# Attention 0 with heads gathered in one PSUM bank, a shared ring of banks and a gated output projection; attention 1 with wide masks and its bias added by GpSimd

## The chip, the cores and the metric

The kernel runs on one core of a Trainium2 chip. The metric is the device time of one launch in microseconds (us), lower is better. TensorE is called PE, VectorE DVE, ScalarE ACT, GpSimd POOL and SyncE SP.

## The reference, cut to what matters

Sixteen batches of 256 tokens with 128 features pass two layers; each layer is an attention and a feed-forward part, both with modulated layer norms and gated residuals. The change lies in the two attentions.

```
mod = (silu(L0_c) @ L0_wmod)...            # sa, ca, ga, sb, cb, gb per batch
h = layernorm(x) * (1 + ca) + sa
q = h @ Wq + bq;  latent = h @ Wl + bl;  k = latent @ Wk + bk;  v = latent @ Wv + bv
attn = softmax(q k^T * 8**-0.5)            # attention 0: 16 heads of 8 features
x = x + ga * (attn v @ Wo + bo)
x = x + gb * ffn0(...)                     # then layer 1:
attn = softmax(causal(q k^T)); A_mem = ... # attention 1: 4 heads of 32 features
x = x + ga1 * ((g * A_mem + (1 - g) * attn v) @ Wo.T + bo)
x = x + gb1 * mixture_of_experts(...)
```

## The kernel before

The program is a row of blocks: `prepare`, `attention0`, the feed-forward part of layer 0, `attention1`, the expert part. Between blocks all engines meet at a barrier. X stays in SBUF.

`attention0` is a software pipeline written by hand. Step n (0 to 19) has 16 slots; each engine runs its own program with the same steps and slots, and the order in it is fixed by the tables `PES`, `DVE` and `ACTS`. In step n the engines work on several batches at once: f = n (layer norm turned by `pe_ln`, projections `pe_qk` and `pe_v`), m = n - 2 (the maxima), s = n - 3 and t = n - 4 (scores, exponentials, values, output). One slot of PE (`pe_tiles`) is one tile of maxima (two matmuls into one of the two banks `p_max`, read by DVE's `dve_max_tile`) and one half of a transposed score tile (two matmuls into `p_sT`, read by ACT's `act_exp`). At slot 0 of step n the maxima's wait asks that the operands of batch n - 2 stand in `QK` (semaphore `stacked`, all 12 transfers of that batch and of those before it).

Those operands are made so: `act_qk` writes q and k, ACT and POOL (`pool_parts`) split them in three bf16 parts, and SP copies the parts from SBUF to SBUF with 12 DMAs of 64 KB (`sp_stack`, the stack of a batch below). The maxima of batch s go the other way round: DVE splits them (`dve_negmax`, slot 0), PE turns them (`pe_max_turn`, slot 2), ACT copies (`act_maxT`), SP copies them into `QK` with 2 DMAs (`sp_max`), and the scores of s, from slot 6 on, need them.

SP's program per step is `sp_max(n - 3)`, one group of feed-forward weights, `sp_stack(n)`. SP is a queue in order: a wait in it holds back all that stands behind it.

The output of batch t: `pe_pv` (four groups of heads, each 4 heads x 2 key tiles, into 4 x 32 partitions of `p_o`), `act_OT` four times, `pe_turn_O` twice, `dve_normalise_O` twice, `pe_turn_back`, `act_OTn`, `pe_out`, `act_y` (gate and bias per feature), `pe_turn_y`, `dve_add`. All but `p_o` share the bank `p_m`.

`attention1` has one step per batch, PE's order being scores, turn_a, out, logits, turn_b, turn_c, mem, q and k, v, pv, layer norm. `pe_out` adds the gated bias with a matmul of one row behind each projection.

Of the kernel before, what the change touches and what calls it, by code (L numbers as in the profile page):

```python
# [22 lines left out]
P = 128  # L23
# [20 lines left out]
PES = {"ln": 0, "max_turn": 2, "qk": 3, "O0": 5, "v": 8, "O1": 9, "back": 11, "out": 12, "turn_y": 14,  # L44
       "pv_s": (11, 15), "pv_t": (3, 7)}
DVE = {"negmax": 0, "stats": 2, "O0": 6, "O1": 10, "add": 15}
ACTS = {"hT": 0, "maxT": 1, "qk": 3, "v": 7, "OTn": 11, "y": 12, "OT_s": (11, 15), "OT_t": (3, 6)}
# [75 lines left out]
def prepare(nc, k, a):  # L123
    with ExitStack() as ctx:
# [24 lines left out]
        zeroed = sem("zeroed")  # L149
        ident_ready = sem("ident_ready")  # L150
# [50 lines left out]
        def _(pool):  # L201
# [8 lines left out]
            for r in range(NB):  # L210
                pool.memset(k.V[r][:, :, :, DH0 + 1:], 0.0)
                if r >= 2:
                    pool.memset(k.QK[r][:, :, 1, :], 1.0)
# [34 lines left out]
        def _(dve):  # L248

            for r in range(NB):  # L250
                dve.memset(k.V[r][:, :, :, DH0:DH0 + 1], 1.0)
                if r < 2:
                    dve.memset(k.QK[r][:, :, 1, :], 1.0)
            dve.wait_ge(small_loaded, SMALL)
# [58 lines left out]
def late_loads(k, a):  # L313
# [4 lines left out]
    loads.append((k.bo1[:], a["L1_attn_bo"].rearrange("(o d) -> o d", o=1)))  # L318
# [11 lines left out]
def attention0(nc, k, a):  # L330
    with ExitStack() as ctx:
        sb, ps, sem = tensors(nc, ctx, "att0")
        QK, V = k.QK, k.V
        stats = sb("stats", [P, NT, 6])
# [13 lines left out]
        OT = [sb(f"OT{n}", [P, S]) for n in range(4)]  # L348
        recip = sb("recip", [P, 2, NT, 4])
        O = sb("O", [P, NT, H0, DH0])  # L350
        OTn = sb("OTn", [P, S])
        yT = sb("yT", [P, S])
# [8 lines left out]
        p_o = ps("p_o", [P, 512])  # L361
        p_m = ps("p_m", [P, 512])
        p_m16 = p_m[:].bitcast(BF16)

        stats_step = sem("stats_step")
# [14 lines left out]
        scored = sem("scored")  # L380
        maxed = sem("maxed")
# [9 lines left out]
        O_turned = sem("O_turned")  # L391
        recip_ready = sem("recip_ready")
        O_ready = sem("O_ready")
        OTn_turned = sem("OTn_turned")
        OTn_ready = sem("OTn_ready")
        y_made = sem("y_made")
        yT_ready = sem("yT_ready")
        y_turned = sem("y_turned")
        x_added = sem("x_added")

# [9 lines left out]
        STACK_DMAS = 2 * len(TERMS)  # L410

# [5 lines left out]

        def head_rows(w, n):
            return slice(w * HALF, w * HALF + n)


        def pe_ln(pe, b):
            pe.wait_ge(xn_ready, b + 1)
            at_least(pe, v_ready, b)
            at_least(pe, x_added, b - 4)
# [4 lines left out]
        def pe_qk(pe, b):  # L430
            pe.wait_ge(hT_ready, b + 1)
            at_least(pe, maxT_ready, b - 2)
            pe.matmul(p_m[:, 0:S], k.wq0[:], hT[:], start=True, stop=True)
            pe.matmul(p_m[:, S:2 * S], k.wk0[:], hT[:], start=True, stop=True).then_inc(qk_made, 1)

        def pe_v(pe, b):
            pe.wait_ge(qk_ready, b + 1)
            at_least(pe, O_ready, 2 * (b - 4) + 1)
# [4 lines left out]
        def pe_tiles(pe, max_of, scores_of):  # L443

            if max_of is not None:
                b, r, u = max_of
                if u == 0:
                    pe.wait_ge(stacked, 16 * STACK_DMAS * (b + 1))
                at_least(pe, maxed, TILES * b + u - 1)
# [6 lines left out]
            for i in range(NT):  # L456
                if max_of is not None:
                    rows = head_rows(w, MAXROW)
                    mm = pe.matmul(p_max[u % 2][:, i, :], QK[r][rows, g, 0, i * P:(i + 1) * P], QK[r][rows, g, 1, :],  # L459
                                   start=True, stop=True)  # L460
                    if i == NT - 1:
                        mm.then_inc(scored, 1)
# [7 lines left out]
        def pe_max_turn(pe, b):  # L470
            pe.wait_ge(neg_ready, b + 1)
            if not isinstance(b, int) or b + 3 < B:
                wait_apart(pe, k, hT_ready, b + 4)
            else:
                at_least(pe, x_added, b - 1)
# [5 lines left out]
        def pe_pv(pe, b, r, g):  # L481
            if g == 0:
                pe.wait_ge(v_ready, b + 1)
            pe.wait_ge(exped, PAIRS * b + 2 * g + 2)
            at_least(pe, OT_ready, 4 * b + g)
            for j in range(NT):
                for h in range(4):
                    mm = pe.matmul(p_o[32 * h:32 * h + 32, 0:S], V[r][:, j, 4 * g + h, :],  # L488
# [391 lines left out]

# [1306 lines left out]
```

## Time and profile before

| | us |
|---|---|
| median of 3 runs | 896.36 (893.45 to 896.53) |
| the profiled execution's own time | 895.1 |
| its span | 893.3 |
| `prepare`, up to about | 21 |
| attention 0, about | 21 to 342 |
| feed-forward 0, about | 342 to 568 |
| attention 1 and its router, about | 568 to 742 |
| experts, about | 742 to 893 |

Over the whole span PE is busy 83%, DVE 69%, ACT 63% and POOL 40%. These are means over stages with different limits; what holds a stage is read from that stage's own rows.

### The profile page before, as it was taken

To read this page: it belongs to the slowest core of one execution; us is meant where nothing else is said; L and a number is where in the kernel's file an instruction comes from. 1 tells how busy PE (TensorE), PEld (TensorE's weight loads), DVE (VectorE), ACT (ScalarE), POOL (GpSimd) and SP (SyncE) were. 2 spreads that over 40 slices of the span, in tenths; PEclk is the share of its full clock that TensorE was granted. 3 is DMA by queue.
4 is the path that set the end of the run, shared out by engine and by line. 5 is a ranking of instruction groups with operands and counts; after the bars stand their busy time and mean duration, and the time that the engine had idled before them with its cause. 6 is when DMAs were issued, how large, how long until landed. Compare 5 with 4: busy or idle time off the path is not lost. (4 is left out here: it accounts for less than half of the span.)

```text
span 893.3 us, 17728 instructions
## 1 busy us (share of the span) xinstructions
PE 743.3 (83%) x5927; PEld 538.4 (60%) x5927; DVE 613.4 (69%) x1483; ACT 563.2 (63%) x1258; POOL 359.6 (40%) x449
## 2 busy tenths in 40 slices
PE   3376888888888874789999997589999967999996
PEld 3222444444444334789889997367777755888784
DVE  3075777777777835677877763367767856888884
ACT  0214777777777753668878886277677734565553
POOL 3542534534421001051121000477877643777674
PEclk9999999999999985899999999599999987999998
DMA  5355354443442001300000000000000060464430
GB/s 138 47 73 73 64 67 66 66 68 52 55 54 41 2 3 14 119 1 2 1 1 1 1 1 1 2 2 1 2 1 3 18 176 4 112 187 114 118 107 23
DMA packets 76927, 42.05 MB, mean 47 GB/s; under 512 B 9026, under 2 KB 74916, under 8 KB 76580
## 3 DMA queue, kind: packets, MB, share of 16 engines
q1 hardware_dynamic: 76836, 40.89, 22.9%
q8 instruction: 51, 0.84, 0.4%
q14 instruction: 40, 0.33, 0.2%
HBM read 25.66 MB, written 2.24 MB: 31 GB/s over the span
## 5 line engine op out<-in xcount | busy, mean ns | idle before, releaser
L579 DVE TENSOR_REDUCE att_negmax<-att_p_max 128x2 f32<-128x512 f32 x256 | 164.6, 685 | 74.2 <-PE att_p_max L459 73.2
L663 ACT ACTIVATE att_probs<-att_p_sT 128x1024 f32<-128x1024 f32 x128 | 129.3, 1022 | 47.1 <-PE att_p_sT L465 46.1
L2047 POOL TENSOR_TENSOR moe_z_lo<-moe_z,moe_z_hi 128x512 fp32r<-128x512 f32 x64 | 96.6, 1524 | 54.8 <-ACT moe_z_hi L2000 53.0
L459 PE MATMUL att_p_max<-att0p_QK 48*128 48x256 bf16 x512 | 91.6, 288 | 26.9 <-DVE att_negmax L579 11.4
L939 POOL TENSOR_TENSOR ffn0s_rstd<-ffn0s_var_eps,top_minus_half 128x2 f32<-128x2 f32 x16 | 11.2, 698 | 197.3 <-DVE ffn0s_var_eps L926 197.3
L465 PE MATMUL att_p_sT<-att0p_QK 51*128 51x256 bf16 x512 | 86.0, 281 | 0.2 <-DMA att0p_QK<-att_maxT 0.2
L893 PE MATMUL ffn0s_p_h<-ffn0s_u_hi,top_ffn_all 128*128 128x256 f32 x256 | 70.9, 309 | 16.5 <-DVE ffn0s_u_lo L1154 16.2
L459 PEld LDWEIGHTS att_p_max<-att0p_QK 48*128 48x128 bf16 x512 | 33.2, 96 | 77.3 <-DVE att_negmax L579 46.8
L488 PE MATMUL att_p_o<-att_probs,att0p_V 128*32 128x256 f32 x1024 | 70.5, 394 | 10.0 <-ACT att_probs L663 9.0
L1154 DVE TENSOR_TENSOR ffn0s_g_lo<-ffn0s_g,ffn0s_g_hi 128x512 fp32r<-128x512 f32 x64 | 49.0, 781 | 42.0 <-ACT ffn0s_g_hi L1098 40.7
L2038 DVE TENSOR_TENSOR moe_z<-moe_act_u,top_ffn_all 128x512 f32<-128x512 f32 x64 | 73.5, 1149 | 2.2
L1751 POOL TENSOR_SCALAR att_prob<-att_prob,att_rsums 128x256 f32<-128x256 f32 (+1 forms) x128 | 56.0, 455 | 38.2 <-DVE att_rsums L1656 38.1
L1094 ACT ACTIVATE ffn0s_g<-ffn0s_p_h,top_ffn_scales 128x256 f32<-128x256 f32 x128 | 54.5, 486 | 23.2 <-PE ffn0s_p_h L894 22.9
L750 POOL TENSOR_TENSOR att_rstd<-att_var_eps,top_minus_half 128x2 f32<-128x2 f32 x16 | 11.5, 719 | 141.0 <-DVE att_var_eps L572 141.0
L894 PE MATMUL ffn0s_p_h<-ffn0s_u_lo,top_ffn_all 128*128 128x256 f32 x256 | 67.0, 294 | 0.0
L893 PEld LDWEIGHTS ffn0s_p_h<-ffn0s_u_hi,top_ffn_all 128*128 128x128 f32 x256 | 52.1, 203 | 22.2 <-DVE ffn0s_u_lo L1154 15.8
L2017 ACT ACTIVATE moe_act_g<-moe_p_g 128x512 f32<-128x512 f32 x64 | 38.3, 599 | 38.6 <-PE moe_p_g L897 38.6
L893 PE MATMUL ffn0s_p_h<-ffn0s_g_hi,top_ffn_all 128*128 128x256 f32 x256 | 62.0, 283 | 0.0
L894 PE MATMUL ffn0s_p_h<-ffn0s_g_lo,top_ffn_all 128*128 128x256 f32 x256 | 60.9, 279 | 0.0
L2033 DVE TENSOR_TENSOR moe_act_u<-moe_act_g,moe_p_u 128x512 f32<-128x512 f32 x64 | 43.6, 681 | 21.4 <-PE moe_p_u L897 18.7
L1098 ACT ACTIVATE ffn0s_g_hi<-ffn0s_p_h,top_ffn_scales 128x256 fp32r<-128x256 f32 x128 | 54.8, 497 | 0.0
L1563 ACT ACTIVATE att_prob<-att_p_s,att_negmax 128x256 f32<-128x256 f32 (+1 forms) x128 | 52.1, 427 | 3.0 <-DVE att_negmax L1669 2.7
(248 smaller groups left out, 2037.5 us busy)
## 6 DMA issues: line engine op xcount, KB each, us to landing
top_ffn_all<-combine SPq DMA_DIRECT2D x32, 512.0 KB, 6.9
att0p_QK<-att_parts SPq DMA_DIRECT2D x192, 64.0 KB
top_X<-in_L_attn_x SPq DMA_DIRECT2D x4, 512.0 KB, 6.9
att_raw<-in_L_ffn_h_w SPq DMA_DIRECT2D x8, 256.0 KB, 2.8
out_x<-top_X SPq DMA_DIRECT2D x8, 256.0 KB, 2.3
top_wo_all<-gates SPq DMA_DIRECT2D x1, 1024.0 KB, 5.2
ffn0s_raw_gu<-in_L_ffn_w SPq DMA_DIRECT2D x1, 1024.0 KB, 8.0
prep_wmod<-in_L_wmod SPq DMA_DIRECT2D x2, 384.0 KB, 3.7
```

The source lines that it names most:

```text
L459: mm = pe.matmul(p_max[u % 2][:, i, :], QK[r][rows, g, 0, i * P:(i + 1) * P], QK[r][rows, g, 1, :], start=True, stop=True)
L465: mm = pe.matmul(p_sT[t % 2][:, sw, i, :], QK[sr][rows, t, 1, i * P:(i + 1) * P], QK[sr][rows, t, 0, :], start=True, stop=True)
L488: mm = pe.matmul(p_o[32 * h:32 * h + 32, 0:S], V[r][:, j, 4 * g + h, :], probs[g % 2][:, h // 2, h % 2, j, :], start=(j == 0), stop=(j == ...
L579: dve.tensor_reduce(negmax[:, :, w, g], p_max[u % 2][:], AX.X, ALU.max, negate=True).then_inc(maxed, 1)
L663: act.activation(probs[g % 2][:, t % 2], p_sT[t % 2][:], ACT.Exp).then_inc(exped, 1)
L893: pe.matmul(out, w_hi, x_hi, start=first, stop=False)
L894: mm = pe.matmul(out, w_hi, x_lo, start=False, stop=last and w_lo_is_zero)
L1094: act.activation(g[q][:, m, :], p_h[q][:, m, :], ACT.Gelu, scale=k.ffn_scales[:, layer, 2 * q + m:2 * q + m + 1])
L1098: ins = act.activation(g_hi[r][:, 2 * q + m, :], p_h[q][:, m, :], ACT.Gelu, scale=k.ffn_scales[:, layer, 2 * q + m:2 * q + m + 1])
L1751: ins = pool.tensor_scalar(prob[b % 2][:, h, at], prob[b % 2][:, h, at], rsums[:, i, h:h + 1], 0.0, ALU.mult, ALU.add)
L2038: dve.tensor_tensor(z[e % RING][:], act_u[e % 2][:], k.cb[u % 2][:, e, :], ALU.mult).then_inc(z_ready, 1)
L2047: pool.tensor_tensor(z_lo[e % RING][:], z[e % RING][:], z_hi[e % RING][:].bitcast(F32), ALU.subtract).then_inc(z_lo_ready, 1)
```

## The change

Attention 0. Two heads now share a block of 32 columns of V: the second one's values stand at columns 8 to 15, their ones at column 17, and two groups of heads are summed into the same PSUM rows, so that `p_o` holds all 16 heads in one bank. One `act_OT`, one `pe_turn_O` and one `dve_normalise_O` replace four, two and two. The two banks `p_max` become a ring that also takes the turned outputs and the projection (semaphores `filled` and `drained` instead of `scored` and `maxed`), so DVE reads all its PSUM data there. The output projection is token-major: Wo times the gate of the batch is prepared ahead (`pool_gate_wo`), the gated bias is added to X by POOL (`pool_bias`), and `act_y` and `pe_turn_y` are gone. The gates go through DRAM once more, in attention 0 (`pe_turn_gates`, `act_gate_rows`, loads of 4 batches in SP's steps 1 to 4). The tables are rewritten: `pe_max_turn` moves from slot 2 to slot 3 and now waits for `OTn_ready`, the scores of s begin at slot 8 instead of 6, the last part of the output moves to a step of its own (y = n - 5), and there are 21 steps instead of 20. SP's step becomes `sp_max(n - 3)`, `sp_stack(n - 1)`, gates, weights (from step 5 on).

Attention 1. `pe_out` loses its bias matmuls, POOL adds the gated bias to X in `pool_norm1`, and each head's mask is one matmul of 256 columns over both diagonal blocks instead of two of 128.

```diff
-PES = {"ln": 0, "max_turn": 2, "qk": 3, "O0": 5, "v": 8, "O1": 9, "back": 11, "out": 12, "turn_y": 14,
-       "pv_s": (11, 15), "pv_t": (3, 7)}
+PES = {"back": 1, "max_turn": 3, "out": 5, "ln": 6, "q": 9, "k": 10, "v": 13, "O": 14,
+       "pv_s": {14: (0, 0), 15: (0, 1)}, "pv_t": {2: (1, 0), 3: (1, 1), 6: (2, 0), 7: (2, 1), 10: (3, 0), 11: (3, 1)}}
+SCORES = 8
...
         def pe_max_turn(pe, b):
             pe.wait_ge(neg_ready, b + 1)
...
+            at_least(pe, OTn_ready, b - 1)
+            pe.wait_ge(v_ready, min(b + 3, B))
...
+        def pe_turn_O(pe, b):
+            at = RING["O", b]
+            pe.wait_ge(OT_ready, b + 1)
+            at_least(pe, drained, at - 1)
+            for i in range(NT):
+                for half in range(2):
+                    mm = pe.transpose(bank(at)[:, i, half * P:(half + 1) * P], OT[:, half, i * P:(i + 1) * P], k.ident[:])
+            mm.then_inc(filled, 1)
...
         def pe_out(pe, b):
+            at = RING["out", b]
             pe.wait_ge(OTn_ready, b + 1)
-            pe.matmul(p_m[:, 0:S], k.wo0[:], OTn[:], start=True, stop=True).then_inc(y_made, 1)
...
+            for i in range(NT):
+                mm = pe.matmul(bank(at)[:, 0, i * D:(i + 1) * D], OTn[:, i * P:(i + 1) * P], k.wo1_all[:, b, :],
+                               start=True, stop=True)
...
+        def dve_normalise_O(dve, b):
...
+            dve.reciprocal(recip[:], groups[:, :, 2 * DH0:2 * DH0 + 2]).then_inc(recip_ready, 1)
...
+            dve.tensor_tensor(O[:].rearrange("p i (m g d) -> p (i m) g d", g=2, d=DH0),
...
+        def act_OT(act, b):
+            act.wait_ge(pv_made, 4 * b + 4)
...
+            act.activation(OT[:], p_o[:], ACT.Copy).then_inc(OT_ready, 1)
...
-        def sp_step(sp, n, r):
+        def sp_step(sp, n):
             if batch_valid(n - 3):
-                sp_max(sp, n - 3, (r - 3) % NB)
-            if 0 <= n - 1 < WEIGHT_GROUPS:
...
+                sp_max(sp, n - 3, (n - 3) % NB)
+            if batch_valid(n - 1):
+                sp_stack(sp, n - 1, (n - 1) % NB)
...
+            g = n - FIRST_GROUP
+            if 0 <= g < WEIGHT_GROUPS:
...
-            if batch_valid(n):
-                sp_stack(sp, n, r)
...
+        def pool_bias(pool, b):
+            x = k.X[:, b * NT:(b + 1) * NT, :]
...
+            pool.tensor_tensor(x, x, k.gbo1_all[:, b, :].unsqueeze(1).to_broadcast([P, NT, D]), ALU.add).then_inc(bias_added, 1)
...
-                pe.matmul(out, OT[b % 2][:, i * P:(i + 1) * P], k.wo1_all[:, b, :], start=True, stop=False)
-                mm = pe.matmul(out, k.ones_row[0:1, :], k.gbo1_row[0:1, b, :], start=False, stop=True)
+                mm = pe.matmul(out, OT[b % 2][:, i * P:(i + 1) * P], k.wo1_all[:, b, :], start=True, stop=True)
```

The order of SP's queue before, around step 8 of attention 0 (QK3 is the stack of batch 7, QK0 that of batch 8; QK1 and QK2 with maxT are the maxima of batches 5 and 6; the names of semaphores of an earlier block are those of numbers used again):

```order
L732 DMA att0p_QK3<-att0_parts1 8x8x512 x2
L712 DMA att0p_QK1<-att0_maxT 3x8x256 [waits prep_s_bo_made,att0_s_maxT_ready]
L712 DMA att0p_QK1<-att0_maxT 3x8x256
L742 DMA att0_raw1<-in_L0_ffn_h2_w 128x512 [waits att0_s_w_lo_ready,att0_s_w_loaded]
L732 DMA att0p_QK0<-att0_parts0 8x16x256 [waits prep_s_wl_turned,prep_s_bv_ready,att0_s_scoredT]
...
L732 DMA att0p_QK0<-att0_parts0 8x8x512 x2
L712 DMA att0p_QK2<-att0_maxT 3x8x256 [waits prep_s_bo_made,att0_s_maxT_ready]
```

And in the changed kernel around its step 9:

```order
L745 DMA att0p_QK3<-att0_parts1 8x8x512 x2
L768 DMA att0_raw0<-in_L0_ffn_h1_w 128x512 [waits att0_s_w_lo_ready,att0_s_w_loaded]
L768 DMA top_ffn_scales<-in_L0_ffn_h2_s 128x4x1
L725 DMA att0p_QK2<-att0_maxT 3x8x256 [waits att0_s_maxT_ready]
L725 DMA att0p_QK2<-att0_maxT 3x8x256
L745 DMA att0p_QK0<-att0_parts0 8x16x256 [waits prep_s_bias_made,att0_s_stacked,att0_s_scoredT]
...
L745 DMA att0p_QK0<-att0_parts0 8x8x512 x2
```

The stack of batch 8 (QK0) stood ahead of the maxima of batch 6 (QK2) and now stands behind them.

The start of a step on PE, in the changed kernel, step 9 (m = 7 in QK3, t = 5 in QK1):

```order
L481 MATMUL att0_p_max1<-att0p_QK3 128x256 [waits att0_s_exped,att0_s_drained,att0_s_stacked]
L487 MATMUL att0_p_sT0<-att0p_QK1 128x256
...
L528 MATMUL att0_p_m<-top_ident,att0_O 128x128 [waits att0_s_v_ready,att0_s_drained]
L528 MATMUL att0_p_m<-top_ident,att0_O 128x128
...
L509 MATMUL att0_p_o<-att0_probs1,att0p_V1 32x256 [waits att0_s_exped]
L509 MATMUL att0_p_o<-att0_probs1,att0p_V1 32x256 x3
L497 MATMUL att0_p_m<-top_ident16,att0_negparts 48x128 [waits att0_s_v_ready,att0_s_OTn_ready,att0_s_neg_ready]
L497 MATMUL att0_p_m<-top_ident16,att0_negparts 48x128
```

The turning of the maxima (L497) has moved behind slot 2, behind the turning back of the output (L528, whose copy by ACT it waits for) and behind half a group of values (L509). Before, the same step began so:

```order
L427 MATMUL att0_p_m<-top_ident,att0_xn 128x128
L459 MATMUL att0_p_max0<-att0p_QK3 128x256 [waits att0_s_exped,prep_s_gate_step,prep_s_bv_ready]
L465 MATMUL att0_p_sT1<-att0p_QK1 128x256
...
L477 MATMUL att0_p_m<-top_ident16,att0_negparts 48x128 [waits att0_s_neg_ready,prep_s_c_tanh]
L477 MATMUL att0_p_m<-top_ident16,att0_negparts 48x128
```

In both, the first maxima matmul of a step waits for the stack of its batch; what moved is when that stack is issued.

## Rows read from the trace of the kernel before

**Rows 1.** Step 9's window, length, busy PE, PEld, DVE, ACT, POOL, PEclk, DMA, GB/s.
```profile
166.66:183.32 16.66, 14.25 (x156) 6.88 (x154) 12.96 (x33) 12.68 (x20) 7.05 (x8) 1.00 0.45 69
```

**Rows 2.** SP's queue in time: start, length, line, what; steps 9 and 10.
```profile
168.54 1.53 SPq L712 DMA_DIRECT2D att0p_QK<-att_maxT  x2
172.65 9.13 SPq L732 DMA_DIRECT2D att0p_QK<-att_parts  x12
185.21 1.53 SPq L712 DMA_DIRECT2D att0p_QK<-att_maxT  x2
```

**Rows 3.** SP's queue in the first steps.
```profile
29.62 8.50 SPq L732 DMA_DIRECT2D att0p_QK<-att_parts  x12
38.16 0.45 SPq L742 DMA_DIRECT2D att_raw<-in_L_ffn_w_w  x1
44.37 8.44 SPq L732 DMA_DIRECT2D att0p_QK<-att_parts  x12
57.98 7.93 SPq L732 DMA_DIRECT2D att0p_QK<-att_parts  x12
66.02 1.96 SPq L712 DMA_DIRECT2D att0p_QK<-att_maxT  x2
72.36 8.53 SPq L732 DMA_DIRECT2D att0p_QK<-att_parts  x12
85.21 1.54 SPq L712 DMA_DIRECT2D att0p_QK<-att_maxT  x2
```

**Rows 4.** SP's own waits, 29 to 90 us: sum, times, longest.
```profile
SPq L732 <- DMA att0p_QK<-att_parts: 11.9, 3, 5.2
```

**Rows 5.** PE in the first steps, where it sat idle for a transfer.
```profile
44.40 0.61 PE L459 MATMUL att_p_max<-att0p_QK 48*128 48x256 bf16 x4 [6.87 <-DMA att0p_QK<-att_parts]
73.02 0.37 PE L459 MATMUL att_p_max<-att0p_QK 48*128 48x256 bf16 x1 [8.01 <-DMA att0p_QK<-att_maxT]
```

**Rows 6.** ACT at the start of step 9.
```profile
167.23 1.02 ACT L663 ACTIVATE att_probs<-att_p_sT 128x1024 f32<-128x1024 f32 x1
168.15 0.36 ACT L656 ACTIVATE att_maxT<-att_p_m 48x256 bf16<-48x256 bf16 x1
```

**Rows 7.** PE's longest idle stretch in the drain.
```profile
314.51 0.29 PE L477 MATMUL att_p_m<-top_ident,att_negparts 128*48 128x128 bf16 x2 [3.47 <-DVE att_negparts L591]
```

**Rows 8.** Windows behind it; the granted clock is the third figure from the end.
```profile
316.00:318.00 2.00, 1.99 (x12) 0.85 (x8) 0.00 (x0) 1.60 (x3) 0.00 (x0) 0.50 0.04 12
320.00:322.00 2.00, 1.95 (x16) 0.85 (x8) 0.00 (x0) 1.07 (x2) 0.00 (x0) 0.50 0.00 0
```

**Rows 9.** DMA strip of 181 to 187 us: busy tenths in 40 slices of 0.15 us.
```profile
DMA  5676656667666584466532110000000000003110
```

**Rows 10.** ACT's maxima copy in step 17, and DVE at the end of attention 0.
```profile
298.25 0.36 ACT L656 ACTIVATE att_maxT<-att_p_m 48x256 bf16<-48x256 bf16 x1
...
340.69 0.27 DVE L797 TENSOR_REDUCE att_lo_flag<-att_lo_row 1x1 f32<-1x128 f32 x1 [2.01 <-DMA att_lo_row<-flag]
```

**Rows 11.** Groups of one step of attention 0: busy us, mean ns | idle before.
```profile
L668 ACT ACTIVATE att_OT<-att_p_o 128x256 f32<-128x256 f32 x4 | 1.5, 378 | 0.4 <-PE att_p_o L488 0.3
L498 PE MATMUL att_p_m<-top_ident,att_OT 128*128 128x128 f32 x8 | 1.3, 286 | 0.3 <-ACT att_qk L642 0.3
L514 PE MATMUL att_p_m<-top_ident,att_yT 128*128 128x128 f32 x2 | 0.4, 300 | 0.1
```

**Rows 12.** POOL groups of one step of attention 1 (639.9 to 649.3 us).
```profile
L1751 POOL TENSOR_SCALAR att_prob<-att_prob,att_rsums 128x128 f32<-128x128 f32 (+1 forms) x8 | 3.5, 457 | 2.0 <-DVE att_rsums L1656 2.0
L1777 POOL TENSOR_TENSOR w_h_lo<-att_hT,w_h_hi 128x256 fp32r<-128x256 f32 x1 | 0.7, 724 | 0.1
```

**Rows 13.** PE in one step of attention 1, in time.
```profile
640.84 0.48 PE L1500 MATMUL att_p_n<-top_gbo_row,top_ones_row 1*128 1x128 f32 x2
641.25 0.61 PE L1421 MATMUL att_p_n<-top_wg,att_hT 128*128 128x8 f32 x4
```

**Rows 14.** Window of one step of attention 1, columns as in Rows 1.
```profile
640.42:649.78 9.36, 9.01 (x85) 7.00 (x84) 6.61 (x28) 6.88 (x25) 7.16 (x14) 1.00 0.01 2
```

More of the change, by code:

```diff
@@ L416, in weights_loaded, with bank @@
             return 16 * sum(len(g) for g in weight_loads[:groups])
+        RING = {}
+        for n in range(LAST):
+            for slot in range(TILES):
+                if slot == PES["out"] and batch_valid(n - 5):
+                    RING["out", n - 5] = len(RING)
+                if slot == PES["O"] and batch_valid(n - 4):
+                    RING["O", n - 4] = len(RING)
+                if batch_valid(n - 2):
+                    RING["max", n - 2, slot] = len(RING)
+        def bank(at):
+            return p_max[at % 2]
         def head_rows(w, n):
@@ L479, in pe_max_turn @@
             mm.then_inc(max_turned, 1)
[L481 to L488, printed above, removed]
-                                   probs[g % 2][:, h // 2, h % 2, j, :], start=(j == 0), stop=(j == NT - 1))
-            mm.then_inc(pv_made, 1)
@@ L517, in pe_step @@
         def pe_step(pe, n, r):
-            f, m, s, t = n, n - 2, n - 3, n - 4
+            f, m, s, t, y = n, n - 2, n - 3, n - 4, n - 5
             rm, rs, rt = (r - 2) % NB, (r - 3) % NB, r
             for slot in range(TILES):
+                if slot == PES["back"] and batch_valid(y):
+                    pe_turn_back(pe, y)
+                if slot == PES["max_turn"] and batch_valid(s):
+                    pe_max_turn(pe, s)
+                if slot == PES["out"] and batch_valid(y):
+                    pe_out(pe, y)
@@ L620, in dve_step @@
-                if slot == DVE["O0"] and batch_valid(t):
-                    dve_normalise_O(dve, t, 0)
-                if slot == DVE["O1"] and batch_valid(t):
-                    dve_normalise_O(dve, t, 1)
+                    neg_chain(dve, s)
+                if slot == DVE["out"] and batch_valid(y):
+                    dve_add(dve, y)
+                if slot == DVE["O"] and batch_valid(t):
+                    dve_normalise_O(dve, t)
                 if batch_valid(m):
@@ L627, in dve_step @@
                     dve_stats(dve, f + 1)
-                if slot == DVE["add"] and batch_valid(t):
-                    dve_add(dve, t)
         def act_hT(act, b):
@@ L843, in _ @@
         def _(pe):
[L844 to L849 removed]
+            pe_turn_gates(pe)
+            for n in range(LAST):
                 pe_step(pe, n, n % NB)
```

379 lines of the change are left out of this document (180 added, 199 removed).

## The prediction

> **What bounds the kernel now.** I read the share of busy time by stage first, then one step of attention 0, then SP's queue, because the change rewrites that queue's order. A step in the steady part lasts 16.66 us and PE is busy 14.25 us of it, DVE 12.96, ACT 12.68 and POOL 7.05 [rows 1]. So PE is the nearest to full, none is full, and a step can be bound by PE's work with DVE's and ACT's short waits, or by a chain that no engine's busy time shows. The reader should look at the transfers next. SP issues the two transfers of the maxima at 168.54 and again at 185.21, which is the period, and between them the 12 transfers of a stack from 172.65, in 9.13 us [rows 2]. In the kernel before, a stack has the rest of its own step and the whole next one before PE wants it, so its flight costs nothing there.
>
> How long a stack flies can be seen where nothing else covers it, at the start. SP issues the first at 29.62; the second waits by its own code for the first to land and leaves at 44.37, the third at 57.98, the fourth at 72.36 [rows 3], and these are the three waits for such a transfer in SP's own waits [rows 4]. PE starts its first maxima at 44.40, released by the same transfers [rows 5]. So a stack takes 14.75, 13.61 and 14.38 us from first issue to landing, mean 14.2, though its issue lasts only 8 to 8.5 us. In each case a group of weights was issued right behind it [rows 3], as it will be in the changed kernel from step 5 on.
>
> **The change, part by part.**
>
> *The stack's place in SP's queue.* Before, step n issues the stack of batch n, wanted at slot 0 of step n + 2. Now step n + 1 issues it, behind the maxima's transfers of that step, wanted again at slot 0 of step n + 2. SP can't issue the stack until ACT has copied the turned maxima. That closes a loop of one step: slot 0, turning of the maxima, ACT's copy, 2 transfers issued, 12 transfers issued and landed, slot 0 of the next step. Its length:
>
> - From slot 0 to the end of ACT's copy. Before, step 9 starts at 166.6, where the window of [rows 1] does, and the copy ends at 168.51 [rows 6]: 1.9 us. Now the turning stands one slot later, behind half a group of values, and waits for ACT's copy of the output, which stands behind an exponential of 1.02 us [rows 6] that itself needs slots 0 and 1. I count: slots 0 and 1 with the turning back 0.9, to the exponential 0.1, exponential 1.0, copy of the output 0.4, turning 0.4, copy of the maxima 0.4: 3.2 us.
> - The two issues, 1.53 us [rows 2], with the gap behind them 1.6.
> - The stack, 14.2 us.
>
> Sum 19.0 us, against 16.67 between the two maxima's issues in [rows 2]. PE's own work is about 13 us in it, so it idles in one piece for 3 us or more. After an idle of 3.47 us in the drain [rows 7] the granted clock stands at 0.50, that is 1.2 instead of 2.4 GHz, in the windows from 316 to 322 [rows 8]. If that happens in every step, slots 0 to 3 take up to 1 us more, in part of the steps. I take 19.2 us for a step.
>
> Bounds of the stack's flight: below, the end of traffic instead of the landing. The strip of 181 to 187 us goes to zero at slice 22 to 27 of 0.15 us, about 184.4 to 185.1 [rows 9], 12.4 us after 172.65; I use 12.6. Above, 15.2, since steps 1 to 4 also load 512 KB of gates behind each stack. I take 14.2 because it is a landing, and the landing is what PE waits for.
>
> The Trainium skill (DMA: Bandwidth & Descriptors, on the two cost components of a transfer) gives a fixed cost of about 2 us for a DMA plus its bytes over 436 GB/s. An estimate by that page lets the last of the 12 transfers land about 2.2 us after its issue, the stack after 10.6 us and the loop after 15.4 us, so nothing would wait for it. In [rows 3] the landing comes 13.6 to 14.8 us after the first issue, so the trace disagrees where it can be seen.
>
> Steps 4 to 16 are 13 steps of the loop. Before, the maxima's transfers of step 4 leave at 85.21 [rows 3], and ACT's copy of step 17 ends at 298.61 [rows 10]: 213.4 us. Now 13 x 19.2 = 249.6. **Plus 36.2 us.**
>
> *The start.* Before, PE sat idle 8.01 us in step 3 for the maxima's transfers [rows 5], since these were issued at 66.02 behind the third stack [rows 3]; that goes. Against it, steps 2 and 3 run the loop too, cold, and the second stack waits for the store and the loads of the gates: about 61 us for step 3's start, 67 for the third stack's issue, 81 to 82 for its landing. Step 4 then issues its maxima's transfers at about 85. **0 us**, between -5 and +2.
>
> *Work taken from PE, ACT and DVE in attention 0.* Half of the 8 turnings, 0.65 us, and the turning of y, 0.4; three of four copies of 378 ns and the scaling, about 1.5 us of ACT; about 0.5 us of DVE [rows 11]. POOL gains a bias add of about 0.73 us (the 128x256 row in [rows 12]), on an engine busy 7 of 16.7. All of it lies beside the loop, so it is worth nothing in steps 4 to 16. If the loop did not bind, it would be worth up to 1.1 us of PE in a step. In the drain there is one step more, but its slots are nearly empty and the chain from last values to X is shorter by the scaling and its turning. Before, the stage ends with the flag at 340.69 [rows 10]. **Minus 1.5 us**, between -3 and +2.
>
> *Attention 1.* A bias matmul pair holds PE from 640.84 to 641.25 [rows 13], 0.41 us, and there are two in each of 16 steps: 13.1 us. PE is busy 9.01 of 9.36 us in a step [rows 14], so it is PE's time. The wide masks give about 0.1 us a step. POOL is busy 7.16 us of 9.36 and waits 2.0 us for DVE; with the add of 0.72 [rows 12, 14] it reaches 7.9 to 8.2, against a step of about 8.5. It stays just behind PE, but it takes part of the gain where it doesn't. DVE's add now waits for POOL's, which is made three steps ahead of it, so that wait is covered; without the lead it would cost at most POOL's 0.7 a step. **Minus 11 us**, between -4 and -14.
>
> Sum: 36.2 + 0 - 1.5 - 11 = +23.7 us. The profiled execution took 895.1 us, 1.3 under the median of the runs; I add the difference to both, and give the median: 896.4 + 23.7, about **920 us**.
>
> **The rivals.**
>
> *The stack is hidden (faster).* If it landed about 2 us after its last issue, the loop would be 4.8 + 10.6 = 15.4 us, and PE and DVE would set about 15.5. Then 13 x 15.5 = 201.5 is 11.9 less than before, and the sum -11.9 - 1.5 - 11 gives 872. It speaks for this that the last part of a stack shared the engines with weights at the start; against it, three landings that agree, and traffic to 12.4 us in the steady part, where no weights were behind the stack. It decides at a flight under 11.9 us, where the loop equals 16.7.
>
> *It lands when traffic ends (no change).* Flight 12.6, step 17.4, 13 steps 226.2, +12.8 - 1.5 - 11: 897.
>
> *PE cold in every step (slower still).* The clock falls in each pause, slots 0 to 3 take 1.2 us more, and gates or weights stretch the stack by 0.3: step 20.5, 266.5, +53 - 1.5 - 11: 937.
>
> *The change's gains in attention 1 don't come* because POOL becomes its bound: -4 instead of -11, 927. It lies in the likeliest one's range.
>
> **How the numbers follow.** The likeliest, the loop with a flight near 14.2 us, has 0.68, and its own range, with the last rival in it, is 908 to 930. The cold one has 0.08, the traffic's end 0.10, the hidden stack 0.14. Leaving out the hidden one and some of the cold one, the range is 895 to 937. A measurement of this kernel tells about 0.5%, 4.5 us, from no change. Slower by more than that: 0.68 + 0.08 + 0.02 of the third, 0.78; within it 0.08; faster 0.14.
>
> **What would show it.** In the profile after, PE's first maxima matmul of each step waits for the stack's transfer, 2 to 5 us, 13 times or so; SP's maxima's issues lie 19 us apart; the stack's first issue comes right behind them and about 4.8 us after PE's slot 0; DVE and ACT wait for PE in one long piece a step, and PE's clock falls in some. A step of attention 1 is 8.5 us. I am wrong if the issues are 16 us apart or less, or if PE's slot 0 waits for something else. That would mean that the landing at the start isn't that of the steady part.

## Result: slower by 3.6%, and the profile after

The changed kernel takes 927.26 us (median of 4 runs, 922.44 to 934.43) against 896.41 for the kernel before on the same chip. The ratio is 1.036, with a 95% interval of 1.028 to 1.044. The profiled execution took 924.53 us, with a span of 922.8 against 893.3. All medians and ranges below are of all runs of a version, but the ratios leave out runs of a slower state, which are five of the ten of the version with half of the stack on GpSimd's queue and one of the four with GpSimd's splitting.

The page of the changed kernel gives the busy times and the strip of PE's granted clock, in tenths, one digit for 1/40 of the span:

```profile
PE 765.3 (83%) x5738; PEld 516.2 (56%) x5738; DVE 633.5 (69%) x1423; ACT 538.8 (58%) x1195; POOL 390.3 (42%) x484
...
PEclk9998886779797886679999999979999996999998
```

PE has 189 matmuls fewer than before and is busy 22 us longer. That is only possible at a lower clock, and the strip says where: mostly in slices 4 to 18 (69 to 415 us), which are attention 0 from its step 3 on and the first 30 us of what follows.

SP's queue shows the step, with the columns of [rows 2]:

```profile
104.42 1.56 SPq L725 DMA_DIRECT2D att0p_QK<-att_maxT  x2
106.09 8.01 SPq L745 DMA_DIRECT2D att0p_QK<-att_parts  x12
...
124.84 1.56 SPq L725 DMA_DIRECT2D att0p_QK<-att_maxT  x2
126.52 8.02 SPq L745 DMA_DIRECT2D att0p_QK<-att_parts  x12
...
144.39 1.55 SPq L725 DMA_DIRECT2D att0p_QK<-att_maxT  x2
```

The maxima leave 20.4 and 19.6 us apart, where [rows 2] had 16.67. PE, where it idles longest in the same steps:

```profile
100.37 0.39 PE L481 MATMUL att_p_max<-att0p_QK 48*128 48x256 bf16 x1 [2.74 <-DMA att0p_QK<-att_parts]
...
120.79 0.39 PE L481 MATMUL att_p_max<-att0p_QK 48*128 48x256 bf16 x1 [3.77 <-DMA att0p_QK<-att_parts]
...
140.34 0.39 PE L481 MATMUL att_p_max<-att0p_QK 48*128 48x256 bf16 x1 [2.90 <-DMA att0p_QK<-att_parts]
```

So the reader can walk round the loop: slot 0 at 100.37, the maxima's issue at 104.42 (4.05 us later), the stack's first issue at 106.09 (1.67), slot 0 at 120.79 (14.70). The next flight, 126.52 to 140.34, is 13.82. In the 13 steps from 84.94 to 339.86 PE's slot 0 is released by the stack 12 times, with flights of 11.82 to 14.78 us, 13.96 in the mean. PE's waits from 30 to 370 us (line, releaser, sum, times, longest) have it first:

```profile
PE att_p_max L481 <- DMA att0p_QK<-att_parts: 43.8, 15, 9.2
PE att_p_max L481 <- DVE att_negmax L597: 13.8, 31, 2.2
```

The windows of four steps and of the drain have the columns of [rows 1]:

```profile
104.42:124.84 20.42, 16.29 (x152) 6.08 (x150) 13.88 (x28) 11.21 (x16) 7.90 (x9) 0.83 0.44 53
124.84:144.39 19.55, 16.29 (x152) 6.07 (x150) 13.87 (x28) 11.20 (x16) 7.89 (x9) 0.85 0.41 56
144.39:167.22 22.83, 20.39 (x152) 7.05 (x150) 15.04 (x28) 11.31 (x16) 7.77 (x9) 0.65 0.40 48
206.99:223.73 16.74, 14.95 (x156) 5.88 (x158) 13.77 (x29) 11.23 (x17) 7.10 (x10) 0.96 0.36 66
339.86:384.92 45.06, 38.46 (x302) 13.06 (x300) 19.25 (x33) 22.12 (x26) 0.00 (x0) 0.72 0.01 2
```

Steps differ: 16.7 us at a clock of 0.96, 22.8 us at 0.65. The short one had the shortest flight, 11.82 us, and its path from slot 0 to the end of the copy at 223.71, 3.24 us, at full clock:

```profile
208.65 8.13 SPq L745 DMA_DIRECT2D att0p_QK<-att_parts  x12
220.47 0.28 PE L481 MATMUL att_p_max<-att0p_QK 48*128 48x256 bf16 x1 [0.95 <-DMA att0p_QK<-att_parts]
```

The long one is the one step of the 13 in which PE doesn't wait for the stack at slot 0, which it reaches at 161.49. Two slots later it waits for VectorE:

```profile
164.83 0.39 PE L481 MATMUL att_p_max<-att0p_QK 48*128 48x256 bf16 x1 [2.24 <-DVE att_negmax L597]
```

The end of attention 0 and the rows of attention 1's step (line 1511 is once in a step):

```profile
384.92 0.27 DVE L833 TENSOR_REDUCE att_lo_flag<-att_lo_row 1x1 f32<-1x128 f32 x1
```

```profile
652.53 0.60 PE L1511 MATMUL att_p_t<-top_ident,att_prob 128*128 128x128 f32 x4
...
660.38 0.60 PE L1511 MATMUL att_p_t<-top_ident,att_prob 128*128 128x128 f32 x4
```

The accounts by stage: attention 0 ends at 384.92, 44.2 us later than in [rows 10]. Of that the 13 steps from the maxima's issue at 84.94 to that at 339.86 give 254.9 - 213.4 = 41.5, and the drain from there on 3.0. Attention 1, from its first to its last row of line 1511, takes 120.1 us against 133.5 before, 13.4 less. The rest is 1.3 less. Sum +29.5, the difference of the spans.

### The profile page after: what moved, and what is told of

Read it like the earlier page. It is cut to its first block and busy times, and to the rows that moved or that the text cites. A ratio compares the mean times of both kernels' runs of the same rounds, so it can differ in the third digit from the quotient of the medians.

```text
span 922.8 us, 17153 instructions
## 1 busy us (share of the span) xinstructions
PE 765.3 (83%) x5738; PEld 516.2 (56%) x5738; DVE 633.5 (69%) x1423; ACT 538.8 (58%) x1195; POOL 390.3 (42%) x484
## 5 line engine op out<-in xcount | busy, mean ns | idle before, releaser
L597 DVE TENSOR_REDUCE att_negmax<-att_p_max 128x2 f32<-128x512 f32 x256 | 172.4, 690 | 97.4 <-PE att_p_max L481 93.3
L481 PE MATMUL att_p_max<-att0p_QK 48*128 48x256 bf16 x512 | 115.6, 325 | 58.6 <-DMA att0p_QK<-att_parts 43.8
L481 PEld LDWEIGHTS att_p_max<-att0p_QK 48*128 48x128 bf16 x512 | 31.0, 100 | 150.3 <-DVE att_negmax L597 61.1
L487 PE MATMUL att_p_sT<-att0p_QK 51*128 51x256 bf16 x512 | 114.5, 324 | 0.0
L509 PE MATMUL att_p_o<-att_probs,att0p_V 128*32 128x256 f32 x1024 | 102.1, 479 | 0.3 <-ACT att_probs L681 0.3
L898 PE MATMUL ffn0s_p_h<-ffn0s_u_hi,top_ffn_all 128*128 128x256 f32 x256 | 69.5, 305 | 16.6 <-DVE ffn0s_u_lo L1159 16.2
L1099 ACT ACTIVATE ffn0s_g<-ffn0s_p_h,top_ffn_scales 128x256 f32<-128x256 f32 x128 | 54.7, 488 | 23.6 <-PE ffn0s_p_h L899 23.2
```

What stands on the lines that cost most here:

```text
L481: mm = pe.matmul(bank(at)[:, i, :], QK[r][rows, g, 0, i * P:(i + 1) * P], QK[r][rows, g, 1, :], start=True, stop=True)
L487: mm = pe.matmul(p_sT[t % 2][:, sw, i, :], QK[sr][rows, t, 1, i * P:(i + 1) * P], QK[sr][rows, t, 0, :], start=True, stop=True)
L509: mm = pe.matmul(p_o[32 * h:32 * h + 32, g // 2, :], V[r][:, j, (g // 2 * 4 + h) * 2 + g % 2, :], probs[g % 2][:, h // 2, h % 2, j, :], st ...
L597: dve.tensor_reduce(negmax[:, :, w, g], bank(at)[:], AX.X, ALU.max, negate=True).then_inc(drained, 1)
L898: pe.matmul(out, w_hi, x_hi, start=first, stop=False)
L1099: act.activation(g[q][:, m, :], p_h[q][:, m, :], ACT.Gelu, scale=k.ffn_scales[:, layer, 2 * q + m:2 * q + m + 1])
```

## Experiments

**Theory**: a step is the loop of the prediction, closed by the stack standing behind the maxima on SP's queue. **Rival A**: the stack's wait is only where PE's idle time shows, and the new order on PE, the ring of two banks, is the slow part. **Rival B**: a stack is slow wherever it is issued. "Steps 4 to 17" below is always the time from ScalarE's copy of the maxima in step 4 to that in step 17, 13 steps: 213.4 us in the kernel before, 254.9 in the changed one.

**The late stack alone, in the kernel before.**

```diff
-            if batch_valid(n):
-                sp_stack(sp, n, r)
+            if batch_valid(n - 1):
+                sp_stack(sp, n - 1, (r - 1) % NB)
```

> The kernel before, with the stack of batch n - 1 instead of n in SP's step n, in the same place behind the maxima's transfers and the weights; nothing else changed. Loop theory: a step becomes 1.9 us to the copy of the maxima, 2.1 for these transfers and the weights' issue, 14.2 for the stack's flight, 18.2 us instead of 16.67. Over 12 to 13 steps that is +18 to +20 us, less up to 5 at the start: 908 to 916 us. Rival, the new slots and the ring make the longer step, not the place of the stack: no change, 896 within 3.

Measured: 904.6 us, ratio 1.011 (1.005 to 1.016): slower, as the loop theory has it, but 3 us under the range that I had given. PE again waits for the stack, in the order of before:

```profile
115.52 0.28 PE L459 MATMUL att_p_max<-att0p_QK 48*128 48x256 bf16 x1 [0.89 <-DMA att0p_QK<-att_parts]
...
149.25 0.28 PE L459 MATMUL att_p_max<-att0p_QK 48*128 48x256 bf16 x1 [0.32 <-DMA att0p_QK<-att_parts]
```

Steps 4 to 17 take 227.6 us, 17.5 each. The prediction's sum with the old path to the copy, 1.9 + 1.6 + 14.2, is 17.7. The 17.5 is a mean of unlike steps: four of the 13 take 16.67 or 16.68 us, with no wait for the stack, and the loop hardly exceeds PE's own step here. The move of one call thus costs 14 us there without any change of PE's order (the start gives 5.7 back, since step 4's copy comes at 79.14 instead of 84.82), and the rest of the 41.5 needs the longer path to the copy, or the clock.

**The stack back in its own step, in the changed kernel** (the same edit reversed), and the same with the parts copied at slot 10 in place of 13.

> The changed kernel with the stack of batch n back in SP's step n (wanted two steps later), all slots and the ring as changed. Loop theory: the stack's flight leaves the loop; but the parts are ready only at slot 13, so the stack's issue ends about 21 us after the step's start and holds back the next maxima's transfers, which the scores at slot 8 want; a step of about 17 us instead of 19.6, 890 to 900 us. Rival, the slots and the ring make the longer step: 927 within 5.

> As the run before, and ACT splits off the first parts at slot 10 instead of 13, so that the stack's issue ends before the next maxima are turned. Loop theory: a step of 15.5 to 16 us, bound by PE and DVE, clock at full level again; 13 x (19.6 - 15.7) = 51 less than the changed kernel, 872 to 882 us. Rival, the slots and the ring: 927 within 5.

Measured: 1006.9 us (ratio 1.127) and 976.9 us (1.091), the opposite of what I expected. SP's queue of the first:

```profile
173.50 8.50 SPq L745 DMA_DIRECT2D att0p_QK<-att_parts  x12
...
183.01 1.55 SPq L725 DMA_DIRECT2D att0p_QK<-att_maxT  x2
199.42 8.51 SPq L745 DMA_DIRECT2D att0p_QK<-att_parts  x12
```

and PE between:

```profile
189.49 0.37 PE L481 MATMUL att_p_max<-att0p_QK 48*128 48x256 bf16 x1 [7.44 <-issue]
```

In this order the parts come at slot 13, so the stack leaves as the step ends, and the next step's maxima stand behind its 12 issues. They leave at 183.01, and PE stands 7.44 us before slot 8, where the scores want them (the profile names no releaser, but that transfer is what the code waits for there). The next parts are behind that slot: another loop, of 25 us. Undoing one line of a change is no undoing, since the slots around it had moved. The two say nothing against the theory, but they show that the queue's order, not the number of transfers, decides.

**Two more transfers between the maxima and the stack, in the changed kernel.**

```diff
+            at_least(sp, spared, 32 * b)
+            for w in range(2):
+                sp.dma_start(spare[w * 3 * PAIRS:(w + 1) * 3 * PAIRS, :], maxT[w * 3 * PAIRS:(w + 1) * 3 * PAIRS, :]
+                             ).then_inc(spared, 16)
```

> The changed kernel, with two more transfers of the maxima's size, into a spare tile that nobody reads, on SP's queue between the maxima and the stack in every step. An issue of the maxima takes 0.8 us, so the stack's first issue comes 1.6 us later. Loop theory: the delay goes round the loop, 1.6 us a step in 13 steps (the two of the start and the drain aside), +21 us and more where the clock falls further: 942 to 960. Rival 'the stack is not what sets the step': 922 to 932, the spread of the changed kernel.

Measured: 954.2 us, ratio 1.066 (1.063 to 1.068), 27 us over the changed kernel and in the range I had given. Steps 4 to 17 take 287.3 us, 22.1 each, 2.5 more for a dose (the added delay of the stack's first issue) of 1.6:

```profile
110.95 1.56 SPq L732 DMA_DIRECT2D att_spare<-att_maxT  x2
112.63 8.04 SPq L752 DMA_DIRECT2D att0p_QK<-att_parts  x12
```

```profile
109.35:131.99 22.64, 16.08 (x152) 6.06 (x150) 13.87 (x28) 11.20 (x16) 7.89 (x9) 0.80 0.39 49
131.99:157.07 25.08, 23.11 (x152) 7.89 (x150) 15.08 (x28) 11.53 (x16) 7.77 (x9) 0.57 0.33 45
```

What stands on the queue ahead of the stack is paid in every step: rival A alone falls. The excess over the dose, 0.9 us a step, is half flight and half clock: over the 12 steps that the stack releases the flight is 14.4 us in place of 14.0, and the path from slot 0 to the copy 4.1 in place of 3.7. The one step without such a release, the second window at 0.57, takes 25.1 us.

**The maxima on ScalarE's queue, in the changed kernel.**

```diff
             act.activation(maxT[:], p_m16[0:6 * PAIRS, 0:S], ACT.Copy).then_inc(maxT_ready, 1)
+            act_max(act, b, b % NB)
...
-            if batch_valid(n - 3):
-                sp_max(sp, n - 3, (n - 3) % NB)
```

> The changed kernel, with the two maxima's transfers issued on ScalarE's queue right behind the copy that makes them, so that SP's queue holds only the stack, the gates and the weights and issues each stack as its parts come, some four slots before slot 0 of the next step. Loop theory: the loop maxima, stack, slot 0, turn is cut, TensorE waits for no stack, its clock stays high, and a step takes TensorE's own 15.3 to 15.8 us in place of 19.6: some 13 x 4 = 52 us under the changed kernel, 868 to 880 us. ScalarE gets two issues of about 0.8 us a step, of which some may show. Rival 'the transfers' flight is what costs, wherever it is issued' (they share the queues and land late): 915 to 930. Rival 'TensorE's new order with single-bank ring is the slow part': 915 to 930 as well, but with TensorE waiting for the ring's reads and not for the stack.

Measured: 910.3 us, ratio 1.014 (1.005 to 1.022). After the first stack (9.2 us) PE waits for one 0.4 us in the whole stage, the loop is cut. But the gain is 17 us, not 52. Step 9's window and PE's waits from 60 to 350 us:

```profile
166.79:183.91 17.12, 14.17 (x152) 5.71 (x152) 13.69 (x28) 11.09 (x17) 7.85 (x10) 1.00 0.47 65
```

```profile
PE att_p_max L481 <- DVE att_negmax L597: 35.2, 48, 2.4
PE att_p_max L481 <- DMA att0p_QK<-att_maxT: 6.4, 1, 6.4
```

Steps 4 to 17 take 236.0 us, and they are of two kinds. Nine in a row, from 132.53 to 284.05, are at full clock and take 16.3 to 17.2 us, 16.8 in the mean, not the 15.3 to 15.8 of my expectation. In step 9's window PE idles 1.24 us before slot 2, behind VectorE's splitting of the maxima at the step's start, and 0.98 before slot 8:

```profile
172.74 0.27 PE L481 MATMUL att_p_max<-att0p_QK 48*128 48x256 bf16 x1 [0.98 <-DVE att_negmax L597]
```

VectorE's reads ahead of that slot had ended by 171.92; what that slot still waits for is the maxima's transfer, issued at 167.20. Where the wait at slot 8 is 0.2 us or less the step is 16.3 us, under the 16.67 of before. So rival A holds little: at full clock the new order isn't slower than the old one, and the ring's wait at slot 2 is a part of what keeps it above PE's own time.

The other four steps take 24.6, 19.4, 20.1 and 20.4 us at clocks of 0.50 to 0.81. They account for two thirds of the missing gain, and with them comes something that the kernel before doesn't show in its steady steps. VectorE splits the maxima in four small operations (the chain), whose second and fourth, subtractions, take 0.19 us there each time. Here the chain runs at the same time as GpSimd's splitting of q and k, and some of its operations are stretched:

```profile
181.84 0.19 DVE L609 TENSOR_TENSOR att_negparts<-att_negrest,att_negparts 128x32 bf16<-128x32 f32 x1
...
300.23 1.20 POOL L801 TENSOR_TENSOR att_parts<-att_rest,att_parts 128x512 bf16<-128x512 f32 x1
300.44 1.03 DVE L609 TENSOR_TENSOR att_negparts<-att_negrest,att_negparts 128x32 bf16<-128x32 f32 x1
...
302.13 0.39 PE L481 MATMUL att_p_max<-att0p_QK 48*128 48x256 bf16 x1 [2.23 <-DVE att_negmax L597]
```

The same operation takes 1.03 us in place of 0.19 and ends 0.04 us after GpSimd's. This happens at three step starts (84, 108 and 300 us); PE's wait at slot 2 is then 2.37, 1.74 and 2.23 us in place of 1.24, its next matmul takes 0.39 us in place of 0.28, and the slow steps are those that hold such a start or follow it. That the stretched chain causes them is not shown, since no run moved GpSimd's operations alone.

**GpSimd splits the maxima**, on top of the last: `neg_chain(dve, s)` becomes `neg_chain(pool, n - 3)` at the step's start, with two buffers for the maxima.

> The maxima on ScalarE's queue as before in this series, and the four small operations that split the maxima in parts moved from VectorE to GpSimd, with two buffers for the maxima. It tests what is left of the step there, 17.14 us against 16.67 in the kernel before. If it is VectorE's chain of 1.5 us at the step's start, at which TensorE's ring waits 1.2 us, the step falls to 16.2 to 16.8 us and the time to 895 to 903; if GpSimd brings the chain too late for the turn at slot 3, the wait moves there and the step is 17 to 18 us, 905 to 925; if the wait for the maxima at slot 8 sets it, the step stays at 17.1 and slot 8 waits longer.

Measured: 927.0 us (920.4 to 938.2), ratio 1.035 (1.030 to 1.040), worse. PE waits for the split parts at the turn instead, and the clock is below full in ten of the 13 steps:

```profile
PE att_p_m L497 <- POOL att_negparts L610: 18.9, 14, 1.5
```

```profile
161.91:183.24 21.33, 19.84 (x152) 7.17 (x152) 12.75 (x24) 11.40 (x16) 8.59 (x14) 0.68 0.38 52
```

This step has no wait for a stack and yet lasts 21.3 us: PE is busy 19.84 of it, with the same work that took 14.17 at full clock. It doesn't tell whether the chain on VectorE set the 17.1 us. The three steps at full clock take 18.3 to 18.4 us, over 1 us more than with the chain on VectorE.

**Half of the stack on GpSimd's queue, in the changed kernel.** GpSimd issues the six transfers of the second half of the rows as soon as it has made the parts; SP keeps the maxima and, behind them, the other six.

```diff
-                    for w in range(2):
-                        rows = slice(w * HALF + n * DH0, w * HALF + (n + 1) * DH0)
-                        sp.dma_start(QK[r][rows], term_source(r, w, n)
-                                     ).then_inc(stacked, 16)
+                    rows = slice(n * DH0, (n + 1) * DH0)
+                    sp.dma_start(QK[r][rows], term_source(r, 0, n)).then_inc(stacked, 16)
+
+        def pool_stack(pool, b, r):
+            pool.wait_ge(part2_ready, b + 1)
...
+                pool.dma_start(QK[r][rows], term_source(r, 1, n)).then_inc(stacked1, 16)
```

> The changed kernel, with six of a stack's twelve transfers (the second half of the rows) issued on GpSimd's queue right behind the parts that it makes, a step earlier; the maxima and the other six stay on SP's queue, the maxima ahead. Loop theory: only six transfers stand behind the maxima, issued in 4 us where twelve took 8. If the flight of 14.2 to 14.7 us is made by the issues, it shortens by about 4 us, the loop closes in 15 us and no longer binds; a step is then the 17.1 us that it takes with the maxima on ScalarE's queue: some 2.5 us a step less than the changed kernel, 890 to 905. If the flight is made by the transfers' bytes on shared rings, it stays above 12 us and the time stays at 915 to 930. If GpSimd's queue issues slowly (over 1 us each) its other work comes late and the time is over 930.

Measured: 893.4 us (881.0 to 903.2), ratio 0.991 (0.988 to 0.994): 34 us under the changed kernel. Against the kernel before (896.1 on that chip) it is level or a little faster, by less than its own spread of 22 us. The profiled execution took 896.2. After the first (7.9 us) PE waits for no stack, and the attention's end is at 360.50 in place of 384.92. Its windows:

```profile
104.62:128.17 23.55, 22.28 (x152) 7.82 (x152) 14.19 (x28) 11.53 (x16) 11.85 (x16) 0.58 0.29 48
128.17:144.50 16.33, 14.11 (x152) 5.69 (x152) 13.69 (x28) 11.18 (x16) 10.46 (x13) 1.00 0.37 62
144.50:163.46 18.96, 17.53 (x152) 6.44 (x152) 13.81 (x28) 11.18 (x17) 12.84 (x17) 0.77 0.38 58
```

A step at full clock is 16.3 to 16.6 us, up to 0.3 less than [rows 1]. Rival B falls as the cause of the wait: the same bytes, half of them elsewhere and earlier, are in time. How long they fly isn't seen, since nothing waits for them. Steps 4 to 17 still take 238.2 us, 18.3 each, because in most the clock is below full.

**The same, with SP's half ahead of the maxima** (the two calls in `sp_step` change places).

> The kernel with six of a stack's transfers on GpSimd's queue, and on SP's queue the other six issued ahead of the maxima in place of behind them. Their parts are ready when the step begins and their issues take 4.0 us, about the time until the maxima are ready, so that neither stands behind the other for long. Loop theory: nothing of the stack stays in the loop through the maxima, and the steps that still waited are 16.3 to 16.6 us at full clock: 875 to 893. Rival from the two kernels with the whole stack in its own step, where the maxima landed only with the stack ahead of them: the maxima come late at slot 8, TensorE waits there 1 to 3 us a step, and the time is 895 to 925.

Measured: 965.5 us, ratio 1.079 (1.073 to 1.086). The rival that I had named is right, and larger than I put it:

```profile
127.83 4.82 SPq L747 DMA_DIRECT2D att0p_QK<-att_parts  x6
132.69 1.53 SPq L728 DMA_DIRECT2D att0p_QK<-att_maxT  x2
```

```profile
140.77 0.29 PE L483 MATMUL att_p_max<-att0p_QK 48*128 48x256 bf16 x1 [3.38 <-issue]
```

SP first waits for the last parts. The maxima behind them are issued only 0.3 us after they are ready (132.38), but slot 8 starts about 8 us after that issue, with two halves of a stack in flight: a loop of 23.1 us.

**The weights ahead of the stack, in the changed kernel.**

> The changed kernel, with a step's group of weights issued ahead of the stack in place of behind it. Loop theory: the weights' issues delay the stack's in the steps that have them (about 8 steps), and would cost their issue time of 1 to 2 us a step, +8 to +16 us; but the late-stack variant of the kernel before had flights of 11.6 to 13.7 us in the steps with the weights ahead, against 14.2 without, so that a shorter flight would give back 1 to 2 us a step. Sum 920 to 935; the flight after the first issue tells: 14 says no effect of the place, 12 to 13 says the weights' place matters.

Measured: 919.4 us (916.4 to 926.0), ratio 1.025 (1.020 to 1.030). The profiled steps 4 to 17 take 259.5 us, 4.6 more than in the changed kernel's profile, while the runs' median is 8 less; the profiled execution was the slowest of its four, 926.0. The runs of both kernels spread over some 10 us, so it tells no more than that the weights' place is worth less than that. The flight of 106.54 to 120.85 is 14.3 us, as with the weights behind.

**Attention 1's part alone, in the kernel before; and of this the bias on GpSimd alone.**

> The kernel before with the part of the change in attention 1 alone (bias added by POOL, wide masks). From the two profiles a step of attention 1 goes from 9.36 to 7.92 us and the stage loses about 13 us: 883 us. If part of that came from attention 0's change (other data in place, clock), less: 886 to 890.

> The kernel before, with attention 1's output bias added on GpSimd from a table gated per batch, and its masks as they were. Both parts together took a step of attention 1 from 9.36 to 7.92 us. By TensorE's own rows the bias matmuls (two of 0.1 to 0.2 us a step) are less than the four mask matmuls that the wide mask saves: bias alone 0.3 to 0.6 us of the 1.44 a step, 887 to 892 us in all. Rival 'the bias matmul carries most since its one-row operand is slow': 880 to 884.

Measured: 877.9 us (ratio 0.980, 0.975 to 0.985) and 883.0 us (0.986, 0.982 to 0.990): the first 5 us under my 883, the second where its rival had it. In the middle of attention 1 line 1508 or 1509 comes every 9.36 us before, every 8.25 with the bias alone and every 7.92 with both. So the bias gives 1.11 us a step and the masks 0.33, the other way round than I had expected. From the first to the last row of that line the stage takes 120.5 us with both parts, 13.0 less than before. The spans differ by 17.6; the other 4.6 lie before and behind these rows, and no run explains them.

**Attention 1's part and the maxima on ScalarE's queue, in the kernel before.**

> The kernel before with attention 1's part of the change, and the maxima's two transfers on ScalarE's queue. In the kernel before the stack is issued a step earlier and TensorE waits for it only at the start (6.9 and 8.0 us): loop theory expects the middle steps unchanged at 16.4 us or 0.2 to 0.8 us longer for ScalarE's two issues: 874 to 888 us against 878 of attention 1's part alone. If SP's queue also held up the kernel before, 860 to 870.

Measured: 878.2 us, ratio 0.979 (0.975 to 0.983), the same as without the queue's change. In the order of before SP's queue holds nothing up in the steady steps. 878 us is the fastest median of all versions, 2.0% under before and 5.3% under the changed kernel. So attention 0's part of the change costs 49 us beside attention 1's part alone; cutting the loop gives back 17 of them with the maxima on ScalarE's queue and 34 with half of the stack on GpSimd's.

## Why the prediction was right

**The sum.** 920 us was forecast and 927 measured, inside the range and inside the likeliest case's own 908 to 930. The mechanism is the forecast one. That the number came so near is in part luck: the loop came out 5.3 us and the drain 4.5 us over their terms, attention 1, the start and the rest 4.0 under.

**The loop.** Forecast 19.2 us a step, measured 19.6. Its order is as forecast: SP's issues 19.6 us apart in the mean, the stack's first issue right behind the maxima, PE's slot 0 released by it in 12 of the 13 steps. One move alone (17.5 us a step in the old order) and the dose (22.1 us) show the loop, and cutting it (no wait for a stack of over 0.4 us after the start in either version that does) confirms it. Cutting it gives back 17 to 19 of the 41.5 us in the profiles, not all of them: nearly all that stays is in steps below full clock. The flight of 14.2 us, taken from three landings at the start, is 13.96 in the mean of 12, but it isn't one figure: it goes from 11.8 to 14.8.

**The path to the copy.** This is the mis-sized term. The 3.2 us, counted from rows at full clock, are right at that clock: 220.47 to 223.71 in the changed kernel. But over the 12 steps that the stack releases the path is 3.7 us in the mean. In six of them it is 4.0 (as 100.37 to 104.40), with PE's first matmul at 0.39 us in place of 0.28, and these are the six behind waits of 2.7 us or more; in the other six, behind waits of 0.6 to 2.6 us, it is 3.2 to 3.6. I had given the clock 0.2 us on average and put "cold in every step" among the rivals; it was 0.5. Path, issues and flight together are 3.70 + 1.68 + 13.96 = 19.34 us: the path 0.3 over its term with the clock's, the issues 0.1 over, the flight 0.2 under.

**The one long step.** The remaining 3.6 of the 5.3 us are a single step, 144.39 to 167.22, that no term of the sum had. PE is cold in it (matmuls of 0.39 and 0.42 us) until 157.5 and has full clock from there to slot 0, which it reaches at 161.49, 15.4 us after the stack's first issue. It then waits 2.24 us for VectorE, whose chain is stretched there too (its last operation takes 1.03 us at 163.14, beside one of GpSimd), and copies the maxima 5.7 us after slot 0. Together 12 x 19.34 + 22.83 is 254.9, 41.5 more than before instead of 36.2.

The Trainium skill (TensorE: Matmul & The Clock Gate, on clock oscillation in real kernels) describes a kernel in which every wait for a transfer lets the clock fall, so that each next tile starts cold. Read so, the 0.8 us would come in every step of this loop. The trace agrees for the six steps behind waits of 2.7 us or more (path 4.0 us), and differs for the other six, which start at full clock.

**The drain.** Forecast -1.5, measured +3.0: its window has the same 302 matmuls in 38.46 us of busy time, at a clock of 0.72. The same window before, from 298.66 to 340.69, had 30.51 us at 0.87. I had looked at its work and not at its clock.

**The start.** Forecast 0, measured -0.3 at the maxima's issue of step 4.

**Attention 1.** Forecast -11, measured -13.4 here and -13.0 alone (rows of line 1509, 120.5 instead of 133.5 us). The bias's 0.82 us a step of PE's time became 1.11, the masks' 0.1 became 0.33. The step is 7.92 us and not 8.5, and GpSimd's bias did not stop it.

**The rival that fell for another reason.** "The stack is hidden" was priced at 15.5 us a step and 872 us. The two versions in which it is hidden take 16.3 to 17.2 and 16.3 to 16.6 us at full clock, and 910 and 893 us. The price left out PE's wait for VectorE in the ring of two banks (1.24 us at slot 2), the wait for the maxima at slot 8, and the clock.

**What stays open.** What makes the clock fall in steps that have no long wait. The version with half of the stack on GpSimd has an idle of 1.27 us before slot 2 ahead of a step at 1.00 (126.95) and one of 1.24 ahead of a step at 0.77 (143.28). Its steps 4 to 17 take 22 us more than 13 steps of 16.6 (238.2 - 215.8), all of it in steps below full clock (one of 21.6 us, from 83.06, has 0.98 on record, though its matmuls take 0.39 us and more until 95.9). Four of its chains on VectorE are stretched, at 79, 100, 228 and 300 us, and its three longest steps, 23.6, 21.6 and 19.2 us, follow three of them; the steps at 0.77 (144.50) and 0.84 (251.66) follow none. So the stretched chain is a likely part of the answer and not the whole of it. It wasn't tried to keep GpSimd's splitting of q and k away from VectorE's chain, nor to win back the 1.2 us at slot 2 with the chain elsewhere than on GpSimd.

## What to carry to other kernels

- When a transfer moves behind another on a queue, write down the loop: what its issue waits for, the flight from first issue to landing as the trace shows it where nothing covers it, and who is released. If the sum is above the step, that sum is the step. Here the move of one call made the loop, and PE's and DVE's busy shares of the span (83% and 69%) stayed the same.
- Order on a queue works both ways. Behind the maxima the stack was late by 3 us a step, ahead of them the maxima were late by 3 to 7 us. What gained most was a second queue for a part, issued by the engine that makes the data, and not another order.
- A change made of two parts should be timed in parts: the one in attention 1 alone is 2% faster than before and was buried under the other, which lengthened attention 0 by 44 us.
- When a step is slow without a long wait, compare one small operation's time between a fast and a slow step. Here VectorE's 0.19 us became 1.03 when GpSimd was at work, and that showed in no sum of busy time.

## What the runs showed of the hardware

- Twelve transfers of 64 KB inside the core, issued in some 8 us, land 11.8 to 14.8 us after the first issue (12 stacks of the changed kernel, 14.0 in the mean). Two small ones of the maxima take at most 5.5 us from their issue to slot 8's start (167.20 to 172.7) with a stack under way on another queue, and about 8 (132.69 to 140.77) behind half of it on the same queue.
- In steps 5 to 17 of the changed kernel PE's first matmul of a step takes 0.39 us after the six waits of 2.74 to 4.70 us and 0.28 after the six of 0.58 to 2.61. It isn't a rule for every kernel here: after 3.38 us, in the version with SP's half ahead, the first one takes 0.29 and the next 0.39. For single steps the granted clock is 0.57 to 0.68, mostly the lower of its two levels (1.2 GHz), though PE is busy 89 to 95% of them: 20.39 of 22.83, 23.11 of 25.08, 22.28 of 23.55 and 19.84 of 21.33 us. The same 152 matmuls take 14.1 to 14.2 us at full clock.
- VectorE's subtraction of 128x32 takes 0.19 us, but 0.53 to 1.03 in 22 cases from 75 to 345 us in the changed kernel and in the versions with two more transfers, with the maxima on ScalarE's queue and with half of the stack on GpSimd's. In each of them an operation of GpSimd had started up to 0.22 us earlier, and VectorE's ended 0.04 or 0.05 us after it. Where VectorE's starts first it keeps its 0.19 (181.84, GpSimd's at 181.85); within 0.01 us of each other both outcomes occur.
- An issue on GpSimd's queue took 0.71 us (six in 4.27 us), on SP's 0.67 (six in 4.03).
